# Seven-product output stage on one core: where VectorE and GpSimd do the sums, and when the weight chunks are prepared

## The chip, the cores and the metric

One core of a Trainium2 chip runs the whole program. The metric is the device time of one execution in microseconds, median of three runs.

## What is computed

One layer over 32 sequences of 64 tokens and 1024 features, all in float32:

```
mixed = einsum('bct,bcd->bdt', x, weights[cond])          # 64x64 mix, chosen per sequence
q, k, v = mixed @ Wq.T, mixed @ Wk.T, mixed @ Wv.T        # 32 query heads, 8 key/value heads, 128 wide
q, k = rmsnorm(q) * gain_q, rmsnorm(k) * gain_k
attn = softmax(q k^T / sqrt(128) + alibi + causal mask);  out = attn v
x = x + out @ Wo.T
x = x + ffn(cond2(x))     # base product, bias, low-rank adapters, and a Fourier term; folded into one weight
```

Float32 accuracy is reached with split operands: each operand is a high part, rounded to the fp32r type, and a low part, the rest. Each product is three matmuls (high by high, high by low, low by high).

## The kernel before, in words

**Blocks and units.** The 2048 tokens are four blocks of 512. A block is a list of units: `kv0 q0 q1 kv1 o0 q2 q3 kv2 o1 q4 q5 kv3 o2 q6 q7 o3 f0 f1`. A kv, q or f unit multiplies four token tiles with one 512-column slice of weights: four steps, each of four quarters of six matmuls. An o unit multiplies one pair of head groups with its part of Wo by Strassen's scheme (Winograd's form): seven products (`OPS`), so seven steps of four quarters. One quarter is 6 matmuls of 512 columns, 1.36 us in the trace. In the text "o1.3" is step 3 of unit o1, and "quarter 5 of o1" is counted from that unit's first matmul.

**Sums of the seven products.** On the left side (the attention output, `quads`) s1 to s4 are made: `s3` and `s2` on VectorE (L1564, L1571), `s1` and `s4` on GpSimd (L1672, L1678). Each step's left factor is then split into `lefts` by ScalarE (`op_hi`) and VectorE (`op_lo`). On the result side ScalarE copies products through `kept` (`v1_out`, `v7_out`, `v1_in`, `u2`), GpSimd adds the second product to both halves of two tiles (`v7_add`, L1690), and VectorE adds four quarters of the result to `acc` (`c11`, `c22`, `c21`, `c12`). On the weight side t1 to t4 (`SUM_AT`, L1582 to L1593) are made once, in block 0, for each of four pairs and both halves c: ScalarE's queue issues four loads to `sums` (L1340), VectorE makes four sums, ScalarE's queue issues four stores to `t_scratch` (L1346). `sums` lies on `lefts`.

**Weight chunks.** Every 128x1024 chunk of weights comes by DMA (SyncE's queue, L875) into one of RAWS = 3 buffers `raw`, and is split into a ring of six slots: high part on ScalarE (`w_hi`, L1121), low part on VectorE (`w_lo`, L1367, 448 of them). A load waits until `w_lo` has left its buffer.

**Norm and attention.** After each kv or q step ScalarE squares the result, VectorE makes `mean` (L1477), GpSimd the power -1/2 (`rstd`, L1666), VectorE `scale` (`qn`, L1494) and for keys `gain` (L1501); TensorE transposes `qn` into `qt_bank` (L1075), VectorE and ScalarE split that, and scores, softmax and values follow some quarters later.

**Order.** Every engine works through its instructions in the order in which a planner lists them; a wait in front holds everything behind it. The planner walks through the matmuls and hangs the other work on due times in quarters (`AT`, `LEFT_AT`, `at`, `later`); what falls due is listed at the next whole quarter, by due time. For instance, after a unit's last step: `mean` 1.3, softmax of the step before 5.5 after its own base (so 1.5 here), `scale` 1.7, transposes 2.8, `q_lo` and `k_lo` 3.9, scores 4.8. `preparations` gives each chunk n the time at which chunk n - 6 has been used for the last time plus 0.3, and at least 1 quarter after the chunk before; `w_lo` follows 0.6 quarters after the quarter at which `w_hi` is listed.

Of the kernel before, what the change touches and what calls it, by code (L numbers as in the profile page):

```python
# [12 lines left out]
ALU = mybir.AluOpType  # L13
# [3 lines left out]
P = 128  # L17
# [9 lines left out]
WIDE = 512  # L27
UNIT_CHUNKS = 4
CHUNK = 1024
RAWS = 3  # L30
SBUF_START, SBUF_END = 16512, 229368
SLOTS = 6
# [34 lines left out]
LEFT_AT = (dict(s3=-9, s2=-3, s1=0.5, s4=2.5, op=(-8, -6, -2, 4.4, 8.4, 12.4, 16.4)),  # L67
# [92 lines left out]
class Order(Plan):  # L160
# [185 lines left out]
    def preparations(self):  # L346
# [285 lines left out]
def build_program(nc, d, out):  # L632
# [3 lines left out]
    with ctx:  # L636
# [39 lines left out]
        score = sb("score", [P, 256])  # L676
        prob = sb("prob", [P, 256])
# [10 lines left out]
        qgain = sb("qgain", [P, HD])  # L688
# [428 lines left out]
        def _(eng):  # L1117
# [10 lines left out]
            for stage, key in order.stages:  # L1128
# [4 lines left out]
                elif stage == "const":  # L1133
                    dst, src = ((ident[:, :], "identity"), (alibi[:, :, :], "alibi"), (bias_eff[:, :], "b_base"),
                                (kgain[:, :], "k_norm_w"), (qgain[:, :], "q_norm_w"), (b2[:, :], "b2"),
# [153 lines left out]
                elif stage == "op_hi":  # L1289
# [41 lines left out]
                elif stage.startswith("t_load"):  # L1331
# [4 lines left out]
                    elif pair > 0:  # L1336
                        w.wait_ge("mm", o_step(0, pair - 1, len(OPS) - 1), 3)
# [23 lines left out]
        def _(eng):  # L1361
# [10 lines left out]
            for stage, key in order.stages:  # L1372
# [78 lines left out]
                elif stage == "gain_both":  # L1451
                    w.wait_ge("const", 8)
                    eng.tensor_tensor(kgain[:, :], kgain[:, :], qgain[:, :], ALU.mult).then_inc(done[stage], 1)
# [111 lines left out]
                elif stage == "s2":  # L1565
# [5 lines left out]
                    eng.tensor_tensor(quad("21"), quad("22"), quad("21"), ALU.subtract).then_inc(done[stage], 1)  # L1571
                elif stage == "op_lo":
# [61 lines left out]
        def _(eng):  # L1634
            w = Waits(eng, order, done)
            for stage, key in order.stages:
# [30 lines left out]
                elif stage == "s1":  # L1667
                    blk, pair = key
                    w.wait_ge("s2", blk, pair)
                    w.wait_ge("op_hi", o_step(blk, pair, 0))  # L1670
                    w.wait_ge("op_lo", o_step(blk, pair, 0))
                    eng.tensor_tensor(quad("11"), quad("11"), quad("21"), ALU.add).then_inc(done[stage], 1)  # L1672
                elif stage == "s4":
                    blk, pair = key
                    w.wait_ge("s2", blk, pair)
                    w.wait_ge("op_hi", o_step(blk, pair, 2))
                    w.wait_ge("op_lo", o_step(blk, pair, 2))
                    eng.tensor_tensor(quad("12"), quad("12"), quad("21"), ALU.subtract).then_inc(done[stage], 1)  # L1678
                elif stage == "v7_add":
                    k, tp = key  # L1680
                    kind, blk, pair, m = step(k)
                    t = tiles_of(blk)[2 + tp]
                    w.wait_ge("v7_out", k, tp)
                    if pair > 0:
                        w.wait_ge("c21", o_step(blk, pair - 1, 5), tp)
                    else:
                        w.wait_ge(f"x{t}", blk)
# [119 lines left out]
```

## Time and profile before

| | us |
|---|---|
| median of 3 runs | 2668.3 (2659.5 to 2669.61) |
| profiled execution | 2667.39 |
| its span, first to last instruction | 2665.6 |
| TensorE busy, share of the span | 2441.8 (92%) |
| VectorE | 1811.7 (68%) |
| ScalarE | 1249.5 (47%) |
| GpSimd | 431.5 (16%) |
| mean granted TensorE clock | 0.976 |

How to read it: matmuls are pipelined, so one row can show a matmul for 0.39 us while the next starts 0.23 us later. What the time hangs on are the stretches in which TensorE does nothing, and those in which its clock is at half. Block 0 runs from 146.8 to 812.6 us, block 1 to 1425.7, block 2 to 2044.5, block 3 to the end; ahead of block 0 the folded weight is made.

### The profile page before, as it was taken

What the parts mean: (1) busy time and instruction counts of PE and PEld (TensorE: products, weight loads), DVE (VectorE), ACT (ScalarE), POOL (GpSimd) and SP (SyncE); (2) the same over time, 40 slices, a digit from 0 to 9 for tenths busy, and PEclk for the clock granted to TensorE, in tenths of its full rate; (3) what the DMA queues carried; (4) which work ended last, traced back from release to release, by engine and by line L of the source; (5) the groups of instructions that cost most, each with busy time, mean ns of one, the idle gap of its engine ahead of it and who ended that gap; (6) DMA issues with size and microseconds to landing.
All of it is one profiled execution on the core that took longest, in us unless ns stands there. A gap on an engine that the chain in (4) does not pass through costs nothing.

```text
span 2665.6 us, 32724 instructions
## 1 busy us (share of the span) xinstructions
PE 2441.8 (92%) x11676; PEld 1995.5 (75%) x11676; DVE 1811.7 (68%) x2830; ACT 1249.5 (47%) x2881; POOL 431.5 (16%) x336
## 2 busy tenths in 40 slices
PE   7989989898899999999899999898989989899988
PEld 5867767676678777777778777777768878787867
DVE  5557768676845767676854777767774686867682
ACT  3235545353524545454633555555542554545450
POOL 0101212120211111111121121112130121212021
PEclk8989999999999999999999999999999999999999
DMA  5261433525343141414234141423243132323241
GB/s 206 103 253 64 167 141 135 190 91 194 128 142 111 64 142 65 141 64 142 95 122 149 64 143 64 133 73 126 73 143 135 64 119 87 119 88 111 95 150 48
DMA packets 88436, 316.13 MB, mean 119 GB/s; under 512 B 12716, under 2 KB 13228, under 8 KB 87124
## 3 DMA queue, kind: packets, MB, share of 16 engines
q1 hardware_dynamic: 70292, 247.14, 27.4%
q10 hardware_dynamic: 10944, 37.54, 3.8%
q0 software_dynamic: 7040, 29.36, 3.0%
q8 instruction: 95, 1.56, 0.2%
q14 instruction: 65, 0.53, 0.1%
HBM read 282.54 MB, written 31.46 MB: 118 GB/s over the span
## 4 chain that ended last, share of the span: by engine, by line
PE 61%; DVE 21%; DMA 6%; issue 6%; ACT 4%; POOL 1%; ACTq 0%; POOLq 0%; DVEq 0%
PE main L926 50%; DVE ring L1367 9%; DMA raw<-in_wo 4%; PE qt_bank L1075 2%; ACT ring L1121 2%; DMA sums<-in_wo 2%; DVE qn L1501 2%; PE s_bank L1091 2%; DVE qn L1494 2%; DVE pt_lo L1557 1%; DVE score L1370 1%; PE pv_bank L1110 1%; PE s_bank L1092 1%; POOL rstd L1666 1%; DVE lefts L1367 1%
## 5 line engine op out<-in xcount | busy, mean ns | idle before, releaser
L926 PE MATMUL main<-ring,act_hi 128*128 128x512 f32 x3584 | 1155.8, 404 | 0.0
L926 PEld LDWEIGHTS main<-ring,act_hi 128*128 128x128 f32 x3584 | 646.4, 190 | 112.8
L926 PE MATMUL main<-ring,act_lo 128*128 128x512 f32 x1792 | 705.4, 394 | 0.0
L926 PE MATMUL main<-ring,lefts 128*128 128x512 f32 x2688 | 655.7, 403 | 45.4 <-ACT main L1121 24.6
L1367 DVE TENSOR_TENSOR ring<-raw,ring 128x1024 fp32r<-128x1024 f32 x448 | 607.1, 1364 | 89.5 <-ACT ring L1121 88.2
L1121 ACT ACTIVATE ring<-raw 128x1024 fp32r<-128x1024 f32 x448 | 473.4, 1061 | 400.7 <-PE main L926 274.4
L926 PEld LDWEIGHTS main<-ring,lefts 128*128 128x128 f32 x2688 | 517.8, 195 | 162.2 <-ACT main L1121 29.7
L1666 POOL TENSOR_TENSOR rstd<-mean,half 128x4 f32<-128x4 f32 (+1 forms) x192 | 179.7, 936 | 1606.8 <-DVE mean L1477 1606.8
L926 PEld LDWEIGHTS main<-ring,act_lo 128*128 128x128 f32 x1792 | 339.1, 189 | 75.4
L1075 PE MATMUL qt_bank<-ident,qn 128*128 128x128 f32 x640 | 108.5, 285 | 119.4 <-DVE qn L1501 62.8
L1243 ACT ACTIVATE sq<-main 128x128 f32<-128x128 f32 x640 | 168.8, 277 | 76.7 <-PE main L926 74.4
L1075 PEld LDWEIGHTS qt_bank<-ident,qn 128*128 128x128 f32 x640 | 76.7, 143 | 166.7 <-DVE qn L1501 79.9
L1367 DVE TENSOR_TENSOR lefts<-quads,lefts 128x1024 fp32r<-128x1024 f32 x112 | 142.2, 1270 | 75.9 <-ACT lefts L1121 75.0
L1370 DVE TENSOR_TENSOR acc<-main,acc 128x512 f32<-128x512 f32 x168 | 114.8, 685 | 100.9 <-PE main L926 100.6
L1557 DVE TENSOR_TENSOR pt_lo<-pt_bank,pt_hi 64x256 fp32r<-64x256 f32 x256 | 107.8, 421 | 93.5 <-ACT pt_hi L1278 91.8
L1121 ACT ACTIVATE qt_hi<-qt_bank 128x512 fp32r<-128x512 f32 x128 | 76.1, 594 | 172.0 <-PE qt_bank L1075 171.6
L1269 ACT ACTIVATE prob<-score 128x256 f32<-128x256 f32 x128 | 53.0, 414 | 213.1 <-DVE score L1536 213.1
L1367 DVE TENSOR_TENSOR qt_lo<-qt_bank,qt_hi 128x512 fp32r<-128x512 f32 x128 | 88.2, 689 | 85.8 <-ACT qt_hi L1121 85.8
L1278 ACT ACTIVATE pt_hi<-pt_bank 64x256 fp32r<-64x256 f32 x256 | 97.1, 379 | 96.9 <-PE pt_bank L1099 95.0
L1494 DVE TENSOR_TENSOR qn<-main,rstd 128x512 f32<-128x512 f32 (+1 forms) x192 | 114.4, 596 | 37.8 <-POOL rstd L1666 37.8
L1243 ACT ACTIVATION_READ_ACCUMULATOR sq<-main 128x1 f32 x640 | 132.7, 207 | 0.0
L1091 PE MATMUL s_bank<-k_t,qt_hi 128*128 128x128 f32 x512 | 116.7, 289 | 11.8 <-issue 9.8
(142 smaller groups left out, 2595.3 us busy)
## 6 DMA issues: line engine op xcount, KB each, us to landing
raw<-in_wq SPq DMA_DIRECT2D x128, 512.0 KB, 4.1
raw<-t_scratch SPq DMA_DIRECT2D x128, 512.0 KB, 3.3
raw<-in_wo SPq DMA_DIRECT2D x96, 512.0 KB, 3.3
raw<-in_wkv SPq DMA_DIRECT2D x64, 512.0 KB, 4.2
sums<-in_wo ACTq DMA_DIRECT2D x32, 512.0 KB, 6.3
t_scratch<-sums ACTq DMA_DIRECT2D x32, 512.0 KB, 4.4
raw<-f_scratch SPq DMA_DIRECT2D x32, 512.0 KB, 4.0
acc<-in_x POOLq DMA_DIRECT2D x16, 512.0 KB, 3.6
```

Of the source, the lines that this page charges most:

```text
L926: mm = eng.matmul(bank, a, b, start=start and n == 0 and m == 0, stop=stop and n == len(terms) - 1 and m == 2, skip_group_check=further)
L1075: mm = eng.transpose(qt_bank[:, tile(h)], norm_tile(k)[:, tile(h)], ident[:, :])
L1091: eng.matmul(s_bank[:, a:a + 2 * SEQ], lh, keys, start=True, stop=False)
L1121: eng.activation(dst, src, ACT.Copy).then_inc(done[stage], 1)
L1243: act = eng.activation(sq[:, tile(h)], norm_bank(k)[:, tile(h)], ACT.Square, accum_out=ssum[:, h:h + 1])
L1278: act = eng.activation(pt_hi[rows_of(b), b, :], pt_bank[rows_of(b), 0:256], ACT.Copy)
L1367: eng.tensor_tensor(dst, src, f32(upper), ALU.subtract).then_inc(done[stage], 1)
L1370: eng.tensor_tensor(dst, a, b, ALU.add).then_inc(done[stage], 1)
L1494: eng.tensor_tensor(heads_of(norm_tile(k)[:, cols], heads), heads_of(norm_bank(k)[:, cols], heads), along(rstd[:, 0:heads], heads), ALU.mu ...
L1501: eng.tensor_tensor(keys, keys, kgain[:, :].rearrange("p (o n) -> p o n", o=1).broadcast_to([P, 2, HD]), ALU.mult).then_inc(done[stage], 1)
L1557: rest = eng.tensor_tensor(pt_lo[rows_of(b), b, :], pt_bank[rows_of(b), 0:256], f32(pt_hi[rows_of(b), b, :]), ALU.subtract)
L1666: eng.tensor_tensor(rstd[:, 0:heads], mean[:, 0:heads], half[:, 0:heads], ALU.pow).then_inc(done[stage], 1)
```

## The change

1. `s1`, `s4` and `v7_add` move from the GpSimd program to the VectorE program, with the same waits and the same operands.
2. Their due times in o0 to o2: `s1` from 0.5 to 2.6, `s4` from 2.5 to 6.6. In o3 they stay (12.8 and 15). `v7_add` is listed 1.5 quarters after `v7_out` instead of right behind it.
3. `preparations` spaces the chunks by at least 1.8 quarters instead of 1.
4. `RAWS` goes from 3 to 4 (one more 128x1024 buffer; `qgain` moves into `score` to make room).
5. The weights' own sums: pair 0 at quarter 0 and, for its second half, 14 (was 11); pair 1 at 28 and 42 of block 0 (was behind o0); pair 2 behind o0 and pair 3 behind o1 (were behind o1 and o2), their halves 19 apart (was 11). Within a half the first sum falls due 6 quarters after its start instead of 4, the stores at 9.7 instead of 8. The waits that guard `lefts` and `sums` follow.

```diff
-RAWS = 3
+RAWS = 4
-LEFT_AT = (dict(s3=-9, s2=-3, s1=0.5, s4=2.5, op=(-8, -6, -2, 4.4, 8.4, 12.4, 16.4)),
+LEFT_AT = (dict(s3=-9, s2=-3, s1=2.6, s4=6.6, op=(-8, -6, -2, 4.4, 8.4, 12.4, 16.4)),
            dict(s3=-4, s2=11.8, s1=12.8, s4=15, op=(-8, -2.8, 3.9, 12.6, 14.9, 16, 18)))
...
-                last = max(free[n - SLOTS] + AT["w_hi"], last + 1)
+                last = max(free[n - SLOTS] + AT["w_hi"], last + 1.8)
...
-        for pair in range(KV_HEADS // 2):
-            self.right_factors(pair)
+        for at, pair in ((0, 0), (28, 1)):
+            self.right_factors(pair, at, 14)
+        for pair in (2, 3):
+            self.right_factors(pair, QUARTERS * (self.first_step["o", 0, pair - 2] + len(OPS)), 19)
...
-    def right_factors(self, pair):
-        start = QUARTERS * (self.first_step["o", 0, pair - 1] + len(OPS) if pair > 0 else 0)
+    def right_factors(self, pair, start, apart):
...
         for c in range(2):
-            self.at(start + 11 * c, 0.5, lambda c=c: loads(c))
+            self.at(start + apart * c, 0.5, lambda c=c: loads(c))
             for i, stage in enumerate(("t1", "t2", "t3", "t4")):
-                self.at(start + 11 * c, 4 + 0.8 * i, lambda c=c, stage=stage: self.add(stage, pair, c))
-            self.at(start + 11 * c, 8, lambda c=c: stores(c))
+                self.at(start + apart * c, 6 + 0.8 * i, lambda c=c, stage=stage: self.add(stage, pair, c))
+            self.at(start + apart * c, 9.7, lambda c=c: stores(c))
...
         self.add("v7_out", k, tp)
-        self.add("v7_add", k, tp)
+        self.later(1.5, lambda: self.add("v7_add", k, tp))
...
+        qgain = score
...
         def _(eng):                       # vector
+                elif stage == "s1":
+                    eng.tensor_tensor(quad("11"), quad("11"), quad("21"), ALU.add).then_inc(done[stage], 1)
+                elif stage == "s4":
+                    eng.tensor_tensor(quad("12"), quad("12"), quad("21"), ALU.subtract).then_inc(done[stage], 1)
+                elif stage == "v7_add":
+                    eng.tensor_tensor(both, both, twice, ALU.add).then_inc(done[stage], 1)
         def _(eng):                       # gpsimd: the same three taken out
```

## Rows read from the trace of the kernel before

**Rows 1.** The page: engines' busy time, and the chain that ended last
```profile
PE 2441.8 (92%) x11676; PEld 1995.5 (75%) x11676; DVE 1811.7 (68%) x2830; ACT 1249.5 (47%) x2881; POOL 431.5 (16%) x336
...
PE 61%; DVE 21%; DMA 6%; issue 6%; ACT 4%; POOL 1%; ACTq 0%; POOLq 0%; DVEq 0%
```
**Rows 2.** Waits of the whole run, TensorE's: total us, times, longest us
```profile
PE qt_bank L1075 <- DVE qn L1501: 62.8, 29, 8.5
PE qt_bank L1075 <- DVE qn L1494: 56.6, 35, 6.4
PE main L926 <- ACT main L1121: 24.6, 12, 3.2
```
**Rows 3.** Waits of TensorE in block 0, 146.8 to 812.6 us
```profile
PE qt_bank L1075 <- DVE qn L1494: 31.1, 11, 6.4
PE qt_bank L1075 <- DVE qn L1501: 24.3, 8, 8.5
PE s_bank L1091 <- issue: 8.0, 5, 2.4
```
**Rows 4.** Waits of TensorE in block 1, 812.6 to 1425.7 us
```profile
PE qt_bank L1075 <- DVE qn L1501: 11.7, 7, 3.3
PE qt_bank L1075 <- DVE qn L1494: 8.5, 8, 1.1
```
**Rows 5.** Groups of instructions with shapes: busy us, mean ns, idle before
```profile
L1367 DVE TENSOR_TENSOR ring<-raw,ring 128x1024 fp32r<-128x1024 f32 x448 | 607.1, 1364 | 89.5 <-ACT ring L1121 88.2
...
L1690 POOL TENSOR_TENSOR acc<-acc,kept 128x1024 f32<-128x1024 f32 x32 | 92.2, 2880 | 165.6 <-ACT kept L1121 165.6
...
L1678 POOL TENSOR_TENSOR quads<-quads 128x1024 f32<-128x1024 f32 x16 | 48.2, 3015 | 0.0
...
L1582 DVE TENSOR_TENSOR sums<-sums,sums 128x1024 f32<-128x1024 f32 x8 | 9.8, 1221 | 20.0 <-DMA sums<-in_wo 20.0
```
**Rows 6.** Line L1501, the keys' gain: duration ns min/median/max
```profile
L1501 DVE TENSOR_TENSOR qn<-qn,kgain x64: 424/425/2162, 167.4 to 2441.3; 128x256 f32<-128x256 f32 x64
```
**Rows 7.** Timeline from kv2 to o1 in block 1: start us, us, engine, line
```profile
1070.76 2.12 DVE L1501 TENSOR_TENSOR qn<-qn,kgain 128x256 f32<-128x256 f32 x1
...
1069.39 3.21 POOL L1678 TENSOR_TENSOR quads<-quads 128x1024 f32<-128x1024 f32 x1
...
1072.94 0.69 PE L1075 MATMUL qt_bank<-ident,qn 128*128 128x128 f32 x2 [3.29 <-DVE qn L1501]
```
**Rows 8.** Windows: sums over eight stretches behind such waits, all at PEclk 0.50
```profile
sum 33.40, PE 30.74 PEld 24.51 DVE 15.14 ACT 12.82 POOL 0.82; mean PE 3.84 PEld 3.06 DVE 1.89 ACT 1.60 POOL 0.10
```
**Rows 9.** Timeline in the middle of o1, block 1
```profile
1095.65 1.06 ACT L1121 ACTIVATE ring<-raw 128x1024 fp32r<-128x1024 f32 x1 [1.77 <-DMA raw<-in_wo]
...
1098.19 4.15 PE L926 MATMUL main<-ring,lefts 128*128 128x512 f32 x17 [1.71 <-ACT main L1121]
```
**Rows 10.** Timeline from q3 to kv2, block 1
```profile
1040.82 1.22 DVE L1367 TENSOR_TENSOR ring<-raw,ring 128x1024 fp32r<-128x1024 f32 x1
...
1042.69 0.66 PE L1075 MATMUL qt_bank<-ident,qn 128*128 128x128 f32 x4 [1.05 <-DVE qn L1494]
```
**Rows 11.** Timeline behind o2 in block 0
```profile
620.58 1.83 ACTq L1340 DMA_DIRECT2D sums<-in_wo  x4
...
632.03 1.22 DVE L1586 TENSOR_TENSOR sums<-sums,sums 128x1024 f32<-128x1024 f32 x1 [4.34 <-DMA sums<-in_wo]
...
636.17 1.11 PE L1075 MATMUL qt_bank<-ident,qn 128*128 128x128 f32 x4 [6.19 <-DVE qn L1494]
```
**Rows 12.** Windows: sums over seven stretches of block 0, all at PEclk 0.50
```profile
sum 40.80, PE 28.45 PEld 22.93 DVE 19.97 ACT 9.53 POOL 4.38; mean PE 4.06 PEld 3.28 DVE 2.85 ACT 1.36 POOL 0.63
```
**Rows 13.** Timeline in o3, block 1
```profile
1332.60 2.64 DVE L1367 TENSOR_TENSOR lefts<-quads,lefts 128x1024 fp32r<-128x1024 f32 x1
...
1335.48 5.03 PE L926 MATMUL main<-ring,lefts 128*128 128x512 f32 x11 [5.01 <-issue]
```
**Rows 14.** Windows over four o stages: span, then PE, PEld, DVE, ACT, POOL busy
```profile
1073.30:1111.90 38.60, 36.89 (x152) 29.97 (x151) 26.07 (x24) 20.74 (x24) 5.37 (x2) 0.93 0.49 161
```

More of the change, by code:

```diff
@@ L687, in build_program @@
         kgain = sb("kgain", [P, HD])
-        qgain = sb("qgain", [P, HD])
         mixidx = sb("mixidx", [1, BATCH], I32)
@@ L1134, in _ @@
                     dst, src = ((ident[:, :], "identity"), (alibi[:, :, :], "alibi"), (bias_eff[:, :], "b_base"),
-                                (kgain[:, :], "k_norm_w"), (qgain[:, :], "q_norm_w"), (b2[:, :], "b2"),
+                                (kgain[:, :], "k_norm_w"), (qgain[:, 0:HD], "q_norm_w"), (b2[:, :], "b2"),
                                 (adidx[:, :], "adapter_of_batch"), (adrow[:, :], "adapter_of_row"),
@@ L1303, in _ @@
                     elif blk == 0:
+                        if pair > 0:
+                            w.wait_ge("mm", order.left_before[k], 3)
                         for i in range(4):
-                            w.wait_ge(f"t_store{i}", pair, 1)
+                            w.wait_ge(f"t_store{i}", min(pair + 1, 3), 1)
                     else:
@@ L1335, in _ @@
                         w.wait_ge(f"t_store{i}", pair, 0)
-                    elif pair > 0:
-                        w.wait_ge("mm", o_step(0, pair - 1, len(OPS) - 1), 3)
+                    elif pair == 1:
+                        w.wait_ge(f"t_store{i}", 0, 1)
+                    elif pair > 1:
+                        w.wait_ge("mm", o_step(0, pair - 2, len(OPS) - 1), 3)
                     else:
@@ L1452, in _ @@
                     w.wait_ge("const", 8)
-                    eng.tensor_tensor(kgain[:, :], kgain[:, :], qgain[:, :], ALU.mult).then_inc(done[stage], 1)
+                    eng.tensor_tensor(kgain[:, :], kgain[:, :], qgain[:, 0:HD], ALU.mult).then_inc(done[stage], 1)
                 elif stage == "gains":
@@ L1571, in _ @@
                     eng.tensor_tensor(quad("21"), quad("22"), quad("21"), ALU.subtract).then_inc(done[stage], 1)
+                elif stage == "s1":
+                    blk, pair = key
+                    w.wait_ge("s2", blk, pair)
+                    w.wait_ge("op_hi", o_step(blk, pair, 0))
+                    w.wait_ge("op_lo", o_step(blk, pair, 0))
+                    eng.tensor_tensor(quad("11"), quad("11"), quad("21"), ALU.add).then_inc(done[stage], 1)
+                elif stage == "s4":
+                    blk, pair = key
+                    w.wait_ge("s2", blk, pair)
+                    w.wait_ge("op_hi", o_step(blk, pair, 2))
+                    w.wait_ge("op_lo", o_step(blk, pair, 2))
+                    eng.tensor_tensor(quad("12"), quad("12"), quad("21"), ALU.subtract).then_inc(done[stage], 1)
+                elif stage == "v7_add":
+                    k, tp = key
+                    kind, blk, pair, m = step(k)
+                    t = tiles_of(blk)[2 + tp]
+                    w.wait_ge("v7_out", k, tp)
+                    if pair > 0:
+                        w.wait_ge("c21", o_step(blk, pair - 1, 5), tp)
+                    else:
+                        w.wait_ge(f"x{t}", blk)
+                    both = acc[:, t, :].rearrange("p (u n) -> p u n", u=2)
+                    twice = kept[:, 1, tp, :].rearrange("p (o n) -> p o n", o=1).broadcast_to([P, 2, WIDE])
+                    eng.tensor_tensor(both, both, twice, ALU.add).then_inc(done[stage], 1)
                 elif stage == "op_lo":
@@ L1666, in _ @@
                     eng.tensor_tensor(rstd[:, 0:heads], mean[:, 0:heads], half[:, 0:heads], ALU.pow).then_inc(done[stage], 1)
[L1667 to L1687, printed above, removed]
-                    both = acc[:, t, :].rearrange("p (u n) -> p u n", u=2)
-                    twice = kept[:, 1, tp, :].rearrange("p (o n) -> p o n", o=1).broadcast_to([P, 2, WIDE])
-                    eng.tensor_tensor(both, both, twice, ALU.add).then_inc(done[stage], 1)
                 elif stage in ("fx_load0", "fx_load1"):
```

## The prediction

> **What bounds the kernel now.** I read the page first: TensorE is busy 92% of the span, VectorE 68%, GpSimd 16%, and the chain that ended last is 61% TensorE and 21% VectorE [rows 1]. So no engine but TensorE is full; what can be won is the time in which TensorE stands, and the half-clock stretches behind its stops. The waits view names three releasers: the transposes of `qn` wait 62.8 us for `gain` and 56.6 us for `scale`, the o steps 24.6 us for a ScalarE copy [rows 2]. The mean granted clock of 0.976 says that half-clock stretches cost (1 - 0.976) x 2665.6 = 64 us more. The same view by block shows where: block 0 has 31.1 + 24.3 us of the two `qn` waits, block 1 8.5 + 11.7 [rows 3, 4]; blocks 2 and 3 are like block 1 (8.5 each for `scale`, 13.3 and 13.4 for `gain`). Then the timelines at each stop.
>
> **Part 1, the end of a kv unit (12 places: kv1, kv2, kv3 of four blocks).** The waits for `gain` in blocks 0 to 3 are 24.3, 11.7, 13.3 and 13.4 us; 13.0 of block 0's belong to part 4, some 1.4 lie elsewhere, so 48 us belong to these units. The timeline shows how they arise: behind the unit's last step VectorE still has low parts of chunks in its queue, one of them (1.22 us) between `mean` and `scale`; then `gain` takes 2.12 us while GpSimd's `s4` runs, and TensorE stands for 3.29 us [rows 7]. The same `gain` takes 0.42 us when nothing disturbs it [rows 6], so 1.7 us of the 3.29 are contention; the other 1.6 are queue. In blocks 2 and 3 `s4` meets the chunk's low part instead (one row of 3.31 us where 1.22 is usual), with a stop of 4.0 us. After the change `s1` and `s4` are on VectorE at quarters 2.6 and 6.6, behind `gain`: the 1.7 go whole. By the due times 12 to 16 of a 16-quarter unit were 13.3, 14.3, 15.3, 16.3 and become 13.3, 15.1, 16.9, 18.7: one low part of 1.22 us leaves the queue ahead of `mean`, one stays between `mean` and `scale` (16.9, listed at 17, its low part at 18), where it half hides under the 0.7 us of `rstd`. Following VectorE's rows from kv2.2 on, `gain` ends 3.7 us earlier: 1.7 of its own contention, 1.2 of the low part, 0.8 of what the step before passes on (its `gain` runs beside `s1`, 2.16 us). That is about when TensorE arrives. I leave 0.5 us per place: 48 - 6 = 42 saved. Behind 8 of the 12 stops TensorE ran at the lower of its two levels (1.2 GHz) for 33.4 us together [rows 8]; it had stood 3 to 4 us before each. A half-clock us does half a us of work, so 16.7 us come back with the stops. Sum: **59 us** (bounds 35, if the contention alone goes and half of the clock, and 65).
>
> The Trainium skill, GPSIMD Engine Reference (table at the top), says that GpSimd's SBUF interfaces are shared with VectorE and contend with VectorE instructions that have two SBUF inputs. The trace agrees: `gain` has two and goes from 0.42 to 2.1 us, and additions out of PSUM keep their 0.68 us beside GpSimd's long sums. Were it otherwise, and the 2.12 us had a cause that stays, part 1 would be 12 x 1.7 = 20 us smaller.
>
> **Part 2, the middle of o0 to o2 (12 places).** TensorE waits 24.6 us in all for `u2` [rows 2]. Ahead of that copy in ScalarE's queue stand a high part that waits 1.77 us for its DMA, and `op_hi` [rows 9]. The chunk in question was due at 16.3 of the o unit and is now due at 17.1, behind `op_hi` (16.4) and `u2` (16.6), and a fourth buffer lets its load start one chunk earlier. Either is enough. Saved: **24 us**, with one half-clock stretch of 3.3 us behind a 3.2 us stop, some 1.7, **26 us** in all (bounds 12 and 26).
>
> **Part 3, the end of q units.** In each of blocks 1 to 3 eight `scale` waits of 1.05 us: 8.5 us a block [rows 4]. A low part of 1.22 us stands between `mean` and `scale`, and `mean` is itself late behind another [rows 10]. With the new pace one of the four low parts moves past `scale`; one still stands between. Shifting the rows of VectorE accordingly brings `scale` forward by 0.9 us. The q7 ones don't count (o3, below): 25 places x 0.9 = **22 us** (bounds 0, if the remaining low part still decides, and 26).
>
> **Part 4, the weights' own sums in block 0.** Behind o2 ScalarE's queue issues four loads at 620.58; VectorE's second sum waits for the last until 632.03, 11.4 us later, with `mean` and `scale` behind it, and TensorE stands 6.19 us [rows 11]. The second halves bunch with the four low parts of the unit's end: 2.33, 0.48 and 2.54 us more. All stops of this kind: pair 0 13.0 us, pairs 1 to 3 34.2, with half clock over 40.8 us, 20.4 lost [rows 12]; 68 us.
> New, for pairs 2 and 3: the first sum is due at 6, behind `scale` (5.7), so the wait for the load no longer holds the transposes. What is late next is `q_lo` (7.9), behind t2 and t3: t2 can start 11.0 us behind the unit's start, `q_lo` ends at 14.0, TensorE wants it at 12.9: 1.2 us instead of 5.5 to 6.4, and in these rows half clock came behind stops of 2.5 us and more. The second halves, at 25 to 28, meet no low parts; three sums between `mean` and `q_lo` still cost some 2 us instead of 5.3. Each pair saves 13 us, 26.
> Pair 0 still starts with cold loads (the last lands 13.9 us after issue): 8.5 us become 7, the second half's 4.5 us with 3.4 of clock nearly go: 9. Pair 1 moves into q1 and kv1, crowded by low parts: 16 us become 11, 5 saved. A new wait: o0's first `op_hi` (due at quarter 56) waits for pair 1's last store, issued at quarter 52 and landed 4 to 8 us later. Behind it in ScalarE's queue are the squares and `k_hi` of kv1, in VectorE's `op_lo`; 4 quarters are 7 us there, so it costs 0 to 1 us. Sum 26 + 9 + 5 less 1 for that wait: **39 us** (bounds 20 and 52).
>
> **Part 5, the four added operations on VectorE.** 64 sums leave GpSimd, where they took 2.6 to 3.0 us, and take about 1.22 us on VectorE, the duration of a same-shaped one [rows 5]: 78 us. Against it stands the contention that goes: 448 low parts of the ring take 1.364 us in the mean [rows 5] where 1.217 is their median, 66 us, and 20 gains 1.7 us more each, 34; some 100 us of VectorE's time. In an o unit VectorE is busy 26.07 of 38.6 us [rows 14]; with four sums more (4.9) and 2.6 less of contention it is 28.3, so 10 us stay free. Each o step's left factor and chunks are ready 5 us or more ahead of use by the due times. Cost: nothing, while that slack stands; without it 1.22 us each.
> In o3 there is no such slack: from quarter 1 to `op_lo` of o3.3 VectorE has hardly a pause, the factor itself takes 2.64 us under contention, and TensorE stands 5.01 us [rows 13]. There the change takes away 4.0 us of contention and adds three sums ahead of that factor (two `v7_add`, and `s1` at 12.8 before 13.4): 3.7 us. Net 0.3, with small gaps in between: **3 us** for four blocks (bounds -8 and 12). The stops move, the end of VectorE's queue doesn't.
>
> **The sum.** 59 + 26 + 22 + 39 + 3 = 149. Five parts with one-sided estimates (what new stops come is seen less well than which go): I take off 5 us for small ones of 0.3 us at the 16 pairs: 144. From the profiled execution, 2667.4 (1 us below the median of the runs, so no correction): **2523 us**, 5.4% less.
>
> **Rivals.**
> (a) *VectorE's queue passes the stops on.* What I followed is one boundary of a kind. At the others a low part, a sum or `s3` may take the freed place; the wait for `gain` keeps 1.6 us of queue (12 x 1.6 = 19), its clock returns by half (8), part 3 gives nothing (22), part 4 half (19), less 5 already taken off: 2523 + 63 = 2586 at worst, about **2565** in the middle. For it: VectorE is at 68% and already the releaser of nearly all waits. Against: the 1.7 us of contention and the moved chunk of part 2 don't depend on it.
> (b) *The even pace is not even where it matters.* One low part still stands between `mean` and `scale`: part 3 fails and part 1 keeps 0.6 us more a place: 2523 + 22 + 7 = **2552**.
> (c) *VectorE becomes the bound in the o units, slower than before.* If low parts that wait for ScalarE hold the sums back, and `v7_add` waits for `v7_out` in the in-order queue with low parts and `op_lo` behind it, VectorE's 28.3 us of work stretch over the 38.1 us that TensorE needs for 168 matmuls. It decides from that point, 10 us of stalls per unit, on. Then each of 16 pairs pays its 4.9 us, 78 us, and parts 1 to 3 are used up by late factors; part 4 alone remains: 2667 + 78 - 39 = **2706**. Against: GpSimd's `v7_add` in the trace waited for `v7_out` as well, and VectorE has pauses of 2 to 2.7 us in each of these stages.
> (d) *The change doesn't do what it says*: contention is gone only if nothing long is left on GpSimd. Left are 16 additions of 2.4 us (`biased_x`), untouched before and after; they are in my sum already.
>
> The Trainium skill, GPSIMD Engine Reference § 3.1, gives 4497 ns for GpSimd and 2293 ns for VectorE for an addition of 2048 elements, a ratio of 1.96. Here the ratio is 2880 to 1221, 2.36, with contention in it. By the page's ratio the sums would cost VectorE 2880 / 1.96 = 1469 ns each (an estimate from that page), 16 us of busy time more, all in the free 10 us of a unit.
>
> **How the numbers follow.** Forecast 0.62, (a) 0.22, (b) 0.11, (c) 0.05. Range: from the upper bounds of parts 1, 3 and 4 together, 23 us below, to rival (a)'s middle and a little over: **2500 to 2578**. Two runs differ by up to 10 us, and a measurement can tell about 0.5%, 13 us, from none. Even (a) at its worst is 3% faster, so faster by over 0.5% 0.95, within 0.02, slower 0.03.
>
> **What would show it.** Part 1: `gain` never over 0.5 us, waits for L1501's successor under 15 us in blocks 1 to 3 together instead of 38. Part 2: no wait of TensorE for ScalarE's copy in o steps. Part 3: waits for `scale` in block 1 under 3 us. Part 4: block 0 at most 25 us longer than block 1, now 53 (665.8 and 613.1). Part 5: low parts of the ring at most 1.23 us outside o3, VectorE's busy time down by 20 to 30 us; o3.3's stop still 4 to 7 us. The clock: 0.99 or more. The prediction is wrong if VectorE's stops for ScalarE grow in the o units, or if new waits for `q_lo` or `prob` show in the q units.

## The result, and the profile after

The changed kernel takes **2496.9 us** (median of 4 runs, 2493.2 to 2499.5), against 2669.0 for the kernel before, run beside it (2659.5 to 2670.7). The ratio is 0.936, interval 0.934 to 0.939: 6.4% less, where 5.4% was forecast (2523 us). The measured time lies 3 us below the range of 2500 to 2578, so the direction and the mechanism held and the size did not. The profiled run has a span of 2494.8 us and a mean granted clock of 0.987; before it was 2665.6 us and 0.976. All that follows compares these two spans: 170.8 us.

The page, engines' busy time and the chain that ended last (answers to [rows 1]):

```profile
PE 2407.1 (96%) x11676; PEld 1984.4 (80%) x11676; DVE 1777.3 (71%) x2894; ACT 1242.0 (50%) x2881; POOL 244.9 (10%) x272
...
PE 85%; DVE 10%; issue 3%; DMA 1%; ACT 1%; ACTq 0%; POOL 0%; POOLq 0%; DVEq 0%
```

TensorE was the chain for 61% of the span and is now for 85%; VectorE's share fell from 21% to 10%. VectorE did 64 instructions more in 34 us less busy time.

TensorE's waits over the whole run (total us, times, longest us), to be laid beside [rows 2]:

```profile
PE main L927 <- issue: 23.9, 6, 5.8
...
PE qt_bank L1015 <- DVE acc L1375: 8.3, 8, 1.6
PE qt_bank L1076 <- DVE qn L1499: 7.9, 8, 3.2
PE s_bank L1092 <- issue: 7.4, 5, 2.4
...
PE qt_bank L927 <- DVE k_t L1372: 5.4, 1, 5.4
```

The wait for `scale` (L1494 before, L1499 now) went from 56.6 to 7.9 us. The wait for `gain` (L1501 before, L1506 now) went from 62.8 us to nothing in this list, and so did the wait for ScalarE's copy `u2` (24.6 us). What leads now is the stop in o3 that was expected to stay. Block 1 alone, the answer to [rows 4]:

```profile
PE main L927 <- issue: 5.8, 1, 5.8
...
PE qt_bank L1076 <- DVE qn L1499: 0.7, 1, 0.7
```

The same by block: windows over blocks 0 to 3, each line span, then busy PE, PEld, DVE, ACT, POOL with counts, granted clock, DMA share, GB/s. First the kernel before, then the changed one.

```profile
146.80:812.60 665.80, 584.84 (x2771) 477.01 (x2771) 458.26 (x705) 301.64 (x706) 109.71 (x76) 0.96 0.42 150
812.60:1425.70 613.10, 576.19 (x2793) 472.69 (x2792) 426.57 (x677) 302.53 (x708) 104.74 (x78) 0.99 0.32 107
1425.70:2044.50 618.80, 577.17 (x2794) 473.50 (x2793) 427.05 (x677) 302.60 (x708) 103.29 (x78) 0.98 0.32 106
2044.50:2665.60 621.10, 572.79 (x2769) 469.20 (x2767) 420.67 (x671) 294.07 (x698) 101.77 (x77) 0.98 0.29 100
```

```profile
147.30:752.10 604.80, 575.56 (x2770) 472.94 (x2769) 450.34 (x722) 300.06 (x706) 58.41 (x60) 0.98 0.46 165
752.10:1331.00 578.90, 567.89 (x2793) 470.60 (x2792) 418.22 (x694) 300.77 (x708) 58.51 (x62) 0.99 0.33 113
1331.00:1909.40 578.40, 567.05 (x2793) 469.88 (x2793) 418.19 (x694) 300.65 (x708) 58.50 (x62) 0.99 0.33 114
1909.40:2494.80 585.40, 565.30 (x2769) 467.69 (x2767) 411.55 (x687) 292.07 (x698) 57.52 (x61) 0.99 0.31 105
```

Block 0 gave 61.0 us, the others 34.2, 40.4 and 35.7. Blocks 1 and 2, 5.7 us apart before, are within 0.5 us of each other now. Block 0 is 25.9 us longer than block 1, where it was 52.7.

Where the 170.8 us came from, added up over the trace, without the 13.7 us before TensorE's first matmul in both: its pauses of more than 0.1 us summed to 199.1 us (111 of them) and now sum to 64.6 (60), 134.4 less. Half clock covered 126.0 us of the span and now covers 66.9. But TensorE stood still in 23.7 and in 10.4 us of that, which are in the pauses already, so it worked at half clock for 102.3 us before and 56.4 after; half of the difference, 22.9 us, is time. Together 157.3. The other 13 us are in neither sum. Most of them fit the way a matmul is drawn: in an undisturbed stretch one with 512 columns is drawn as 0.39 us while the next starts 0.227 us after it, so the pause drawn before a stop's first matmul is some 0.16 us shorter than what the stop costs, about 8 us for the 51 pauses that went. That last step is argued from the rows, not shown by a run.

**The end of a kv unit.** Timeline from kv2 to o1 in block 1 (start us, us, engine, line; in brackets the idle time before it), the place of [rows 7]:

```profile
993.65 0.17 DVE L1482 TENSOR_SCALAR mean<-ssum 128x2 f32<-128x2 f32 x1
...
994.60 1.23 DVE L1372 TENSOR_TENSOR ring<-raw,ring 128x1024 fp32r<-128x1024 f32 x1 [0.46 <-ACT ring L1122]
...
996.19 0.43 DVE L1506 TENSOR_TENSOR qn<-qn,kgain 128x256 f32<-128x256 f32 x1
996.53 1.22 DVE L1582 TENSOR_TENSOR quads<-quads 128x1024 f32<-128x1024 f32 x1
...
996.67 0.44 PE L1076 MATMUL qt_bank<-ident,qn 128*128 128x128 f32 x2
```

`gain` takes 0.43 us, `s1` (L1582) follows it on the same engine, and the transposes start with no idle time before them; there were 3.29 us. The low part between `mean` and `scale` is still there. The o units behind it, 43.7 to 49.0 us long before, are 38.5 us in all twelve places.

**The end of a q unit.** Timeline from q3 to kv2 in block 1, the place of [rows 10]:

```profile
968.71 1.22 DVE L1372 TENSOR_TENSOR ring<-raw,ring 128x1024 fp32r<-128x1024 f32 x1
...
969.84 0.68 DVE L1499 TENSOR_TENSOR qn<-main,rstd 128x512 f32<-128x512 f32 x1
...
970.58 0.66 PE L1076 MATMUL qt_bank<-ident,qn 128*128 128x128 f32 x4
```

Here too one low part is left ahead of `scale`, and the 1.05 us stop is gone: units q1, q3 and q5 went from 32.6 to 31.4 us in blocks 1 to 3.

**Block 0** keeps stops of pairs 0 and 1: 5.4 us at 161.4, where the low part of kv0's keys stands behind `t3` (L1618), and this behind `t1` and `t2` (L1611, L1615), which both waited for their loads, and 2.4 and 3.2 us in q1 and kv1. The first, with VectorE's rows:

```profile
161.23 1.23 DVE L1611 TENSOR_TENSOR sums<-sums,sums 128x1024 f32<-128x1024 f32 x1 [2.48 <-DMA sums<-in_wo]
163.97 1.23 DVE L1615 TENSOR_TENSOR sums<-sums,sums 128x1024 f32<-128x1024 f32 x1 [1.51 <-DMA sums<-in_wo]
165.22 1.22 DVE L1618 TENSOR_TENSOR sums<-sums,sums 128x1024 f32<-128x1024 f32 x1
166.37 0.42 DVE L1372 TENSOR_TENSOR k_t<-qt_bank,k_t 128x256 fp32r<-128x256 f32 x1
...
166.84 0.47 PE L927 MATMUL qt_bank<-mixw_hi,x_odd 128*128 128x128 f32 x1 [5.43 <-DVE k_t L1372]
```

**o3** in block 1, the place of [rows 13]:

```profile
1235.42 1.22 DVE L1576 TENSOR_TENSOR quads<-quads 128x1024 f32<-128x1024 f32 x1
1236.55 1.22 DVE L1372 TENSOR_TENSOR ring<-raw,ring 128x1024 fp32r<-128x1024 f32 x1
1237.68 0.69 DVE L1375 TENSOR_TENSOR acc<-main,acc 128x512 f32<-128x512 f32 x1
1238.29 1.22 DVE L1582 TENSOR_TENSOR quads<-quads 128x1024 f32<-128x1024 f32 x1
1239.42 1.22 DVE L1372 TENSOR_TENSOR lefts<-quads,lefts 128x1024 fp32r<-128x1024 f32 x1
...
1240.85 8.53 PE L927 MATMUL main<-ring,lefts 128*128 128x512 f32 x24 [5.81 <-issue]
```

The left factor takes 1.22 us instead of 2.64, but `s1` (L1582) stands right ahead of it, and the stop is 5.8 us instead of 5.0. The experiments say which edit lengthened it: with the sums moved alone it is 4.7 us, with the old pace in the changed kernel 4.7 as well, and it is the even pace that adds the 1.1 us.

### The profile page after: what moved, and what is told of

It reads as the page before. It is cut to its first block, busy times and chain, and to the rows that moved or that the text cites. A ratio compares the mean times of both kernels' runs of the same rounds, so it can differ in the third digit from the quotient of the medians.

```text
span 2494.8 us, 32612 instructions
## 1 busy us (share of the span) xinstructions
PE 2407.1 (96%) x11676; PEld 1984.4 (80%) x11676; DVE 1777.3 (71%) x2894; ACT 1242.0 (50%) x2881; POOL 244.9 (10%) x272
## 4 chain that ended last, share of the span: by engine, by line
PE 85%; DVE 10%; issue 3%; DMA 1%; ACT 1%; ACTq 0%; POOL 0%; POOLq 0%; DVEq 0%
PE main L927 72%; DVE ring L1372 3%; PE qt_bank L1076 3%; PE s_bank L1092 2%; PE pv_bank L1111 2%; PE s_bank L1093 2%; DVE score L1375 2%; PE pt_bank L1100 1%; DVE qn L1499 1%; PE pt_bank L927 1%; PE s_bank L927 1%; PE qt_bank L927 1%; DVE peak L1535 1%; DMA sums<-in_wo 1%; DVE pt_lo L1562 0%
## 5 line engine op out<-in xcount | busy, mean ns | idle before, releaser
L927 PE MATMUL main<-ring,lefts 128*128 128x512 f32 x2688 | 636.8, 395 | 24.0 <-issue 23.9
L1372 DVE TENSOR_TENSOR ring<-raw,ring 128x1024 fp32r<-128x1024 f32 x448 | 556.9, 1244 | 80.0 <-ACT ring L1122 78.5
L927 PEld LDWEIGHTS main<-ring,lefts 128*128 128x128 f32 x2688 | 507.6, 190 | 131.9 <-issue 27.1
L1695 POOL TENSOR_TENSOR rstd<-mean,half 128x4 f32<-128x4 f32 (+1 forms) x192 | 174.7, 910 | 1694.6 <-DVE mean L1482 1694.6
L1372 DVE TENSOR_TENSOR lefts<-quads,lefts 128x1024 fp32r<-128x1024 f32 x112 | 136.7, 1221 | 26.8 <-ACT lefts L1122 24.5
L1499 DVE TENSOR_TENSOR qn<-main,rstd 128x512 f32<-128x512 f32 (+1 forms) x192 | 114.6, 597 | 33.7 <-POOL rstd L1695 33.7
L1122 ACT ACTIVATE lefts<-quads 128x1024 fp32r<-128x1024 f32 x112 | 118.5, 1058 | 27.6 <-PE main L927 20.2
```

What stands on the lines that cost most here:

```text
L927: mm = eng.matmul(bank, a, b, start=start and n == 0 and m == 0, stop=stop and n == len(terms) - 1 and m == 2, skip_group_check=further)
L1122: eng.activation(dst, src, ACT.Copy).then_inc(done[stage], 1)
L1372: eng.tensor_tensor(dst, src, f32(upper), ALU.subtract).then_inc(done[stage], 1)
L1499: eng.tensor_tensor(heads_of(norm_tile(k)[:, cols], heads), heads_of(norm_bank(k)[:, cols], heads), along(rstd[:, 0:heads], heads), ALU.mu ...
L1695: eng.tensor_tensor(rstd[:, 0:heads], mean[:, 0:heads], half[:, 0:heads], ALU.pow).then_inc(done[stage], 1)
```

## The experiments

Three rounds each. The kernel before, run beside them, had medians of 2676.4 us (first four kernels), 2674.6 (next four) and 2677.7 (last four), so ratios are compared, and an interval of 0.005 is 13 us. "Worth" is the distance in ratio, times 2669 us. The kernel before, beside which the change was measured, had 2669.0, so the ratios of the later kernels are up to 0.3% lower for that alone, which makes "worth" larger for a part alone and smaller for a part taken back; nothing shows that the other kernels moved with it. The last column is therefore the span of the profiled run (2665.6 before).

| kernel | us | ratio (interval) | worth | span |
|---|---|---|---|---|
| the change | 2496.9 | 0.936 (0.934 to 0.939) | | 2494.8 |
| **one part alone, against before** | | | | |
| sums moved to VectorE | 2576.2 | 0.962 (0.959 to 0.965) | 101 | 2577.7 |
| sums left on GpSimd, 8 columns wide | 2572.2 | 0.961 (0.957 to 0.964) | 105 | 2571.1 |
| even pace | 2584.9 | 0.965 (0.962 to 0.969) | 92 | 2581.1 |
| weights' own sums ahead | 2653.2 | 0.992 (0.989 to 0.995) | 22 | 2649.9 |
| fourth buffer | 2630.4 | 0.981 (0.978 to 0.984) | 52 | 2632.2 |
| **one part taken back, against the change** | | | | |
| sums back on GpSimd | 2571.4 | 0.961 (0.959 to 0.963) | -66 | 2575.9 |
| old pace | 2544.5 | 0.951 (0.950 to 0.953) | -41 | 2538.3 |
| weights' own sums as before | 2522.1 | 0.943 (0.941 to 0.945) | -18 | 2521.7 |
| three buffers | 2499.8 | 0.935 (0.932 to 0.938) | 3, nothing measurable | 2498.3 |
| **beyond the change** | | | | |
| o3's order | 2491.8 | 0.930 (0.927 to 0.932) | | 2488.8 |
| o3, left factor first | 2489.5 | 0.929 (0.926 to 0.931) | | 2486.5 |
| the same, pair 1 later | 2487.7 | 0.928 (0.926 to 0.931) | | 2481.1 |

The four parts alone add up to 267 us, taken back one by one to 122; together they gave 171. By the spans it is some 221 alone and 155 taken back. Both are what overlapping causes look like: a stop that any one of two edits removes is counted twice in the first sum and never in the second.

### Moved sums alone

```diff
-LEFT_AT = (dict(s3=-9, s2=-3, s1=0.5, s4=2.5, ...
+LEFT_AT = (dict(s3=-9, s2=-3, s1=2.6, s4=6.6, ...
-        self.add("v7_add", k, tp)
+        self.later(1.5, lambda: self.add("v7_add", k, tp))
```

and `s1`, `s4` and `v7_add` in VectorE's program as in the change.

> The kernel before with part 5 of the change alone: the three sums on VectorE at their new due times; pace 1, three buffers, the weights' sums as before. If the contention is what makes gain take 2.1 us: gain at most 0.5 us everywhere, the stops at the ends of the kv units shrink by 1.7 us and those one step earlier (0.52) go, 12 x 2.2 = 26 us, some 10 us of clock with them, o3 3 to 7 us; the stops of 1.05 us at the ends of q units and those in the middle of the o units stay: 2668 - 40 = 2628 us. If VectorE's added 78 us come on the path (rival c), 2660 us or more.

Measured: 101 us saved by the ratio (88 by the span), where 40 were expected. Its rows of TensorE's waits, beside [rows 2]:

```profile
PE qt_bank L1075 <- DVE qn L1494: 54.0, 35, 6.3
PE qt_bank L1075 <- DVE qn L1501: 24.3, 17, 8.2
```

The wait for `gain` falls from 62.8 to 24.3 us although the pace is the old one: outside block 0 the stops at kv ends are 0.5 to 1.7 us, where they were 3.1 to 4.0. The `scale` waits, 1.05 us each in q units, stay. The wait for `u2` falls from 24.6 to 2.0 us in 3 places, with three buffers and the old due times. So the stops of part 2 also had the contention in them, which the prediction had put down to the chunk's place and its load.

### The contention alone

```diff
-  eng.tensor_tensor(quad("11"), quad("11"), quad("21"), ALU.add)
+  eng.tensor_tensor(quad("11")[:, :, :, 0:1], quad("11")[:, :, :, 0:1], quad("21")[:, :, :, 0:1], ALU.add)
```

and likewise `s4` and `v7_add`, all still on GpSimd.

> The kernel before, the three sums left on GpSimd but cut to 8 columns each (that part of the computation is left out), so neither contention nor added work on VectorE. It gives the price of the contention alone. Expected: as the moved sums, plus what they cost VectorE: if they hide in o0 to o2 and cost only o3 3.6 us a block, 2628 - 14 = 2614 us; if they cost 1.22 us each on the path, 2628 - 78 = 2550 us.

Measured: 105 us, level with the moved sums (101). This is the direct price of GpSimd's long sums: what the move gives is their absence, and the 78 us of work that VectorE takes over costs 4 us within an uncertainty of some 9. The trace shows one place for it: the o3.3 stop is 3.6 us here and 4.7 with the sums moved. Rival (c), VectorE as the bound of the o units, is out.

### The pace alone

```diff
-                last = max(free[n - SLOTS] + AT["w_hi"], last + 1)
+                last = max(free[n - SLOTS] + AT["w_hi"], last + 1.8)
```

> The kernel before with the spacing of 1.8 quarters alone. Forecast's steps: the twelve waits for u2 go (24.6 us and 2 of clock), the 1.05 us stops at the ends of q units go (25 to 29 of them, 25 to 35 us), the ends of kv units win 1.2 us each (14 us and some 8 of clock): 2668 - 75 = 2593 us. If one remaining low part between mean and scale still decides (rival b), the 1.05 us stops stay and it is 2668 - 45 = 2623 us.

Measured 2584.9: 92 us less by the ratio, 84 by the span, where 75 were expected. The wait for `u2` is 2.7 us in 8 places. Waits of TensorE, and the end of kv1 in block 1:

```profile
PE qt_bank L1075 <- DVE qn L1501: 41.5, 26, 8.3
...
PE qt_bank L1075 <- DVE qn L1494: 25.3, 10, 5.2
```

```profile
913.70 2.92 POOL L1678 TENSOR_TENSOR quads<-quads 128x1024 f32<-128x1024 f32 x1
914.31 0.41 DVE L1494 TENSOR_TENSOR qn<-main,rstd 128x256 f32<-128x256 f32 x1
914.76 2.13 DVE L1501 TENSOR_TENSOR qn<-qn,kgain 128x256 f32<-128x256 f32 x1
...
916.95 0.44 PE L1075 MATMUL qt_bank<-ident,qn 128*128 128x128 f32 x2 [1.86 <-DVE qn L1501]
```

The `scale` waits fall from 35 to 10: the 1.05 us stops go with the pace alone, so rival (b), one remaining low part that still decides, falls. At the kv ends 1.86 us are left, which are the contended `gain`, 2.13 instead of 0.42. This is the split of part 1 (1.7 contention, 1.6 queue), seen from the other side. The pace has a price that the prediction did not see: the o3.3 stop is 6.8 us in blocks 1 to 3 where it was 5.0.

### The weights' own sums alone

```diff
-        for pair in range(KV_HEADS // 2):
-            self.right_factors(pair)
+        for at, pair in ((0, 0), (28, 1)):
+            self.right_factors(pair, at, 14)
+        for pair in (2, 3):
+            self.right_factors(pair, QUARTERS * (self.first_step["o", 0, pair - 2] + len(OPS)), 19)
```

with the new places and waits of loads, sums and stores, as in the change.

> The kernel before with the new order of the weights' own sums alone (part 4). Blocks 1 to 3 unchanged; block 0 shorter by the 39 us of the forecast's step: 2629 us. With pace 1 the sums meet four low parts at a unit's end instead of three, so pair 1 in q1 and kv1 may cost some us more: up to 2640 us.

Measured 22 us, with an uncertainty of 8. Block 0 is 645.3 us long instead of 665.8, so the part is worth 20 us alone, below the 28 to 39 expected. Contention and the old pace stay in this kernel; that they are the reason isn't shown by it.

### The fourth buffer alone

```diff
-RAWS = 3
+RAWS = 4
...
+        qgain = score
```

> The kernel before with a fourth buffer alone. The forecast said that either the later chunk or the fourth buffer is enough to free u2 in the middle of the o units: 24 us and some clock, 2644 us. If the chunk's due time ahead of u2 still decides, because its raw data come late for another reason, nothing: 2668 us.

Measured 52 us by the ratio, 33 by the span, 32 of them in o0 to o2, where 24 and some clock were expected. No wait of TensorE for `u2` is left at all. The stops at the kv ends become 3.0 us in every block, where they were 3.1 to 4.0. So three edits remove part 2's stops, or nearly so, each of them alone; in the run with the narrow sums there are none either.

### The sums back on GpSimd

The change, with `s1`, `s4` and `v7_add` in GpSimd's program, at the change's due times. In VectorE's and then GpSimd's program:

```diff
-                elif stage == "s1":
...
-                    eng.tensor_tensor(quad("11"), quad("11"), quad("21"), ALU.add).then_inc(done[stage], 1)
...
+                elif stage == "s1":
...
+                    eng.tensor_tensor(quad("11"), quad("11"), quad("21"), ALU.add).then_inc(done[stage], 1)
```

> The changed kernel with the three sums back on GpSimd at the new due times. GpSimd takes them as soon as they are free, so they fall on gain again: 12 x (1.9 + 0.5 + 0.3) = 33 us, some 5 of clock, o3 3 us a block (12): 2547 us. Stops for u2 don't return, as the chunk stays behind u2 and there are four buffers; if contention alone makes them, they do, and it is 2570 us.

Measured 2571, the rival's number, but not by the rival's way: no stop for `u2` shows. The timeline at the end of kv2 in block 1, VectorE, GpSimd and TensorE:

```profile
1024.88 2.41 POOL L1677 TENSOR_TENSOR quads<-quads 128x1024 f32<-128x1024 f32 x1
1024.91 3.45 DVE L1372 TENSOR_TENSOR ring<-raw,ring 128x1024 fp32r<-128x1024 f32 x1 [0.45 <-ACT ring L1122]
...
1027.23 3.33 POOL L1683 TENSOR_TENSOR quads<-quads 128x1024 f32<-128x1024 f32 x1
1028.29 0.41 DVE L1499 TENSOR_TENSOR qn<-main,rstd 128x256 f32<-128x256 f32 x1
1028.73 2.11 DVE L1506 TENSOR_TENSOR qn<-qn,kgain 128x256 f32<-128x256 f32 x1
...
1030.90 0.69 PE L1076 MATMUL qt_bank<-ident,qn 128*128 128x128 f32 x2 [3.81 <-DVE qn L1506]
```

The due times of `s1` and `s4` lie behind `gain`, but nothing else stands ahead of them in GpSimd's queue. It starts `s1` as soon as `rstd` is done and what it waits for is there, and `s4` right behind it. `s1` meets the low part (3.45 us instead of 1.22), `s4` meets `gain` (2.11 instead of 0.43), and TensorE stands 3.8 us at each of the 12 kv ends: 46.2 us in 13 waits. Around 11 of them the clock is at half, 130 us of it in this kernel against 67 in the change. The expectation had 2.7 us a place and 5 us of clock; both were too small. A due time is only a place in a queue, and on an engine that is idle it delays nothing.

### The old pace in the changed kernel

```diff
-                last = max(free[n - SLOTS] + AT["w_hi"], last + 1.8)
+                last = max(free[n - SLOTS] + AT["w_hi"], last + 1)
```

> The changed kernel with the chunks' spacing back at 1 quarter. The 1.05 us stops at the ends of 29 q units should return at 1.2 us each (35 us), 0.7 us at each of 12 kv ends (8), and in block 0 the sums meet four low parts again (some 10): 2497 + 53 = 2550 us. If the pace mattered through the DMAs or u2 as well, stops of TensorE for ScalarE's copy return and it is 2570 us.

Measured 2544.5, close to the expected 2550. TensorE's first wait:

```profile
PE qt_bank L1076 <- DVE qn L1499: 38.9, 33, 3.7
```

The 1.05 us stops are back, and the o3.3 stop falls from 5.8 to 4.7 us.

### The old place of the weights' own sums in the changed kernel

```diff
-        for at, pair in ((0, 0), (28, 1)):
-            self.right_factors(pair, at, 14)
-        for pair in (2, 3):
-            self.right_factors(pair, QUARTERS * (self.first_step["o", 0, pair - 2] + len(OPS)), 19)
+        for pair in range(KV_HEADS // 2):
+            self.right_factors(pair)
```

with the old places and waits of loads, sums and stores.

> The changed kernel with the weights' own sums in their old order. Block 0's excess over block 1 goes from 26 us back to that of the run with the pace alone, 54: 2497 + 28 = 2525 us; by the forecast's part 4 (39) it would be 2536 us.

Measured 2522. Its stops in block 0 are 8.0 and 4.5 us for pair 0, then 6.9, 6.3 and 5.6 us behind o0, o1 and o2 with a second one of 2.5 us each: close to [rows 11] and to what the prediction listed. They add up to 39 us, half clock not counted. The change keeps 5.4, 2.4, 3.2 and 2.2 us. Block 0 is 53.3 us longer than block 1, against 25.9 in the change: 27 us for the order of these sums, as expected here, and not the 39 of the forecast.

### Three buffers in the changed kernel

```diff
-RAWS = 4
+RAWS = 3
```

> The changed kernel with three buffers instead of four. The forecast's step (the moved due time is enough by itself) and the theory from the move alone (u2 was late because a contended low part of 3.4 us freed its buffer late) both expect no stop for u2: 2497 to 2500 us. If the fourth buffer carries part 2, 24 us return: 2521 us.

Measured 2499.8: no difference that can be told. No stop for `u2` comes back.

### The order in o3

```diff
-  dict(s3=-4, s2=11.8, s1=12.8, s4=15, op=(-8, -2.8, 3.9, 12.6, 14.9, 16, 18)))
+  dict(s3=-4, s2=11.8, s1=14, s4=15, op=(-8, -2.8, 3.9, 12.6, 14.9, 16, 18)))
```

and the last pair's `v7_add` later by 8 quarters instead of 1.5.

> The changed kernel with s1 of o3 due at 14 instead of 12.8 and both v7_add of o3 eight quarters behind v7_out, so that the three moved sums stand behind the left factor of o3.3 instead of ahead of it. The forecast charged 3.6 us a block for them. VectorE's chain then waits for the last heads (2.1 us earlier than s2 starts now) and s1 is out of it (1.1): the stop of 5.8 us shrinks by some 3.0, 4 x 3.0 = 12 us, and up to 13 us of half clock with it: 2472 to 2485 us. If the chain is bound elsewhere, 2497 us.

Measured 2491.8 us. The stop falls from 5.8 to 4.1 us, not to the 2.8 expected. With three sums out of the way something else is late, which the next kernel shows.

### o3 with the left factor ahead

The same, with `s2` at 11.5 and the factor of o3.3 at 11.7.

> As the run before it, and the left factor of o3.3 listed at 11.7 instead of 12.6, s2 at 11.5 instead of 11.8: it passes one low part (1.1 us) and one addition to acc (0.6). The stop falls to about 1 us a block and its half clock goes: another 4 x 1.8 = 7 us and what is left of 13 us of clock: 2460 to 2468 us.

Measured 2489.5; the stop is 3.6 us. VectorE, ScalarE and TensorE in block 1:

```profile
1231.74 0.58 ACT L1122 ACTIVATE quads<-pv_bank 128x512 f32<-128x512 f32 x1
...
1233.13 0.69 DVE L1375 TENSOR_TENSOR acc<-main,acc 128x512 f32<-128x512 f32 x1
1233.74 1.22 DVE L1576 TENSOR_TENSOR quads<-quads 128x1024 f32<-128x1024 f32 x1
1234.98 1.06 ACT L1122 ACTIVATE lefts<-quads 128x1024 fp32r<-128x1024 f32 x1 [1.31 <-DVE quads L1576]
...
1236.07 1.23 DVE L1372 TENSOR_TENSOR lefts<-quads,lefts 128x1024 fp32r<-128x1024 f32 x1 [1.12 <-ACT lefts L1122]
...
1237.51 1.92 PE L927 MATMUL main<-ring,lefts 128*128 128x512 f32 x6 [3.63 <-issue]
```

`s2`, the high part and the low part now follow one another with hardly a gap: 1.22, 1.06 and 1.23 us. This is a chain of dependences, not a queue, and a further reordering can win only what stands ahead of `s2`. The stop is 0.5 us shorter than in the kernel above, where 1.8 were expected.

### Pair 1 later

```diff
-        for at, pair in ((0, 0), (28, 1)):
-            self.right_factors(pair, at, 14)
+        for at, apart, pair in ((0, 14, 0), (31, 12, 1)):
+            self.right_factors(pair, at, apart)
```

on top of the kernel above.

> As the run before it, and the weights' own sums of pair 1 at 31 and 43 instead of 28 and 42, so that they stand behind q_lo in q1 and mostly behind scale in kv1. The stops of 2.3 and 3.2 us in block 0 should fall to some 1 us together, with 5 us of half clock: 8 us less than the run before, 2455 us; if the later store of pair 1 holds o0's first left factor, nothing is won.

Measured 2487.7, span 2481.1 us. The stops around pair 1 become 1.1, 1.6 and 2.2 us instead of 2.4 and 3.2: spread, hardly less. It is the fastest of all, 0.8% under the change by the ratios, 0.5% by the profiled spans and 0.4% by the medians. Against the kernel above it the medians differ by 1.8 us, which the spread of four runs doesn't tell from none; of the 5.4 us in the spans, half clock that was 8 us shorter is 4. The expected 2455 was far too hopeful.

## Why the prediction came out as it did

**What held.** Four of the five steps went the way they were worked out. `gain` is never over 0.43 us (at most 0.5 was asked). No wait for `gain` is in TensorE's list of block 1 (blocks 1 to 3: under 15 us was asked). No wait for `u2` is left. Block 1 waits 0.7 us for `scale` (under 3). o3.3's stop is 5.8 us (4 to 7). Part 5's claim that o0 to o2 hide VectorE's added work is shown by the run with the narrow sums: 4 us for 78 us of work. Rivals (a) to (c) did not come, and (d) was no more than its price in the sum: 12 low parts still meet `biased_x`, and the mean of all 448 is 1.244 us, the others' median 1.219. Pairs 2 and 3 keep stops of 2.2, 0.5, 1.1, 0.6 and 1.1 us, none with half clock behind it; 1.2 us and some 2 us a pair were forecast. VectorE's busy time fell by 34 us, a little more than the 20 to 30 asked.

**What failed is the size, and it failed on one side.** 144 us were forecast, 171 came. The steps that were mis-sized are the allowance of part 1, the 0.9 us a place of part 3, o3's term in part 5 and the 5 us taken off at the end. By part:

| part | forecast | came | how it is read |
|---|---|---|---|
| 1 and 2 | 59 + 26 | 98 | o0 to o2 87.4 us shorter, and some 10 for small stops in the kv units and q0 |
| 3 | 22 | 29 | 1.26 us a q unit, as much in the kv units, 23 places |
| 4 | 39 | 37 | the rest of kv0, kv1 and q0 to q7 in block 0 |
| 5, o3 | 3 | 7 | o3 from 63.8 to 64.5 us down to 61.8 to 62.5 |
| taken off for unseen stops | -5 | 0 | |

- *Part 1, "I leave 0.5 us per place"* (6 us): TensorE found no idle time at all there, as the kv timeline shows. The row followed had said "about when TensorE arrives"; the allowance was put on top of a reading that needed none.
- *Parts 1 to 3, their upper bounds* (65 + 26 and 26 us): both were passed. They were sums of drawn pauses, and a pause drawn 0.16 us short at each place (36 and 23 of them) would be 9 us. The q units gave 1.26 us where 0.9 was forecast and 1.05 was the bound.
- *Part 2's "Either is enough"* was nearly right (the pace alone leaves 2.7 us) and incomplete. With the contention gone, hardly anything of either is needed (2.0 us and none are left). It cost the forecast nothing, since the stops vanish once.
- *Part 4* came out near its sum, and within a microsecond or so in pair 0 (8 us saved, 9 forecast) and pair 1 (10.6 us left, 11 forecast), counted as the forecast counts. But it took half of all 40.8 us at half clock for lost, and TensorE worked in only 28.45 of them [rows 12]: 6 us are counted twice. In the same way 16.7 us in part 1 should be 15.4 [rows 8]. And the order of these sums alone is worth 27 us in the changed kernel; the rest of the 37 comes with the other edits.
- *Part 5, o3*: the net of 0.3 us at the stop is what the sums moved alone gave (5.0 to 4.7). That the even pace adds 1.1 us there was in no term, and neither was the 1.4 us stop for `prob` behind q7, which went. That stop was contention too. GpSimd's `v7_add`, VectorE's `prob` and the stop in block 1 before:

```profile
1321.18 2.37 POOL L1690 TENSOR_TENSOR acc<-acc,kept 128x1024 f32<-128x1024 f32 x1 [10.93 <-ACT kept L1121]
...
1321.88 1.95 DVE L1551 TENSOR_TENSOR prob<-prob,inv 128x256 f32<-128x256 f32 x1
...
1323.89 0.44 PE L1099 MATMUL pt_bank<-ident,prob 128*128 128x128 f32 x2 [1.80 <-DVE prob L1551]
```

  One `prob` in each block takes 1.95 us instead of 0.42, and TensorE waits 1.4 to 1.8 us for it. Neither happens in any kernel with the sums moved or narrow; with the sums back on GpSimd both are there again, in three blocks. The prediction listed only `gain` and the low parts as what GpSimd's sums meet.
- *"I take off 5 us for small ones"* came from no row, and the new stops it stood for were not there.

So 11 of the 27 us are cautions, both in the same direction (6 for the places of part 1, 5 at the end), some 2.5 are what part 3 let stand of its stops, 4 are o3, and about 10 are time that drawn pauses do not show. The range repeated the fault. Its lower end of 2500 was the upper bounds of parts 1, 3 and 4; part 5's own upper bound and the 5 us taken off were left out of it. With them it would have begun at 2486.

**The clock** is 0.987, not 0.99 or more. Half clock fell by 59 us, but 27 us of what remains stand behind the o3.3 stops, which the forecast had kept, and 19 at the program's start and end. The criterion didn't follow from the forecast's own terms. **Block 0** is 25.9 us longer than block 1, against 25 allowed: pairs 0 and 1.

**What stays open.** Why the stop at q7's end is 0.7 us where the other q units have 0.1 wasn't followed. That most of the missing 13 us are the drawn ends of matmuls is argued from spacing; no kernel separates it, and some 5 us are in no sum at all.

## What to carry to other kernels

A short job on an idle engine isn't free when that engine shares something with a busy one: first look for a row that is longer than its median, then for what runs on the neighbour at that time. Before moving such a job by due time, ask whether its queue holds anything else, since on an empty queue it runs as soon as its operands allow. When stops have several causes, take back each edit from the finished kernel and also try it alone. And state allowances for the unseen on both sides, and carry every term of the sum into the range.

## What the hardware showed that was not expected

**A meeting of VectorE and GpSimd is a turn, not a slowdown.** The prediction took 2.12 us for `gain` as a price of contention. The rows say more. In the kernel with the sums back on GpSimd, `s1` runs from 1024.88 to 1027.29, its usual 2.4 us, and the low part that began behind it ends at 1028.36, 1.07 us after `s1`. `s4`, begun before that, ends 2.20 us behind the low part, at 1030.56, and `gain` 0.28 us behind `s4`, at 1030.84. With the pace alone, `s4` ends at 916.62 and `gain` at 916.89. So whichever began first runs undisturbed, and the other does its work when the first has ended. The price of a meeting is what is left of the other's instruction: 2.2 us for that low part, 1.7 for that `gain`. Instructions of VectorE with an operand in PSUM (0.41 us at 1028.29, beside `s4`) are not touched.

The Trainium skill, SBUF — State Buffer ("SBUF: two separate sides"), calls the shared pair "an **exclusive lock**, not a bandwidth split", held by the first for the whole instruction, if VectorE's has two SBUF inputs. The trace agrees, in all four meetings above.

**The same stop, two lengths of half clock.** Behind the 5.8 us stops of o3 half clock lasted 6.8 us in every block. Behind stops of 3.6 to 4.4 us in the same place of the last kernels it lasted 3.4 us in some blocks and 6.8 in others, and the 24 stops of 1.05 us in blocks 1 to 3 of the kernel with the old pace were followed by none of it. A stop of about 4 us cost up to 3.4 us more than itself.
